# Turning the attention probabilities of the token stage by DMA, as fp16 halves, instead of on TensorE

## What is computed

```python
enc = one_hot(token_ids, 512) + sinusoidal_pe(256, 512)
def layer(enc, ws):
    wq, wk = ws                                   # 512 x 128 each
    q, k = enc @ wq, enc @ wk
    sims = einsum('bqd,bkd->bqk', q, k) / sqrt(128)
    attn = softmax(where(causal_mask, -1e9, sims), axis=-1)
    return einsum('bqk,bkd->bqd', attn, enc), None
enc, _ = lax.scan(layer, enc, (Wq, Wk))           # 4 layers
h = enc
h = h + rwkv_block(layernorm(h))
```

## Time and profile before

| | |
|---|---|
| runs | 2318.48, 2318.91, 2320.64 us |
| profiled execution | 2319.82 us, span 2317.8 us |
| TensorE busy | 2238.2 us, 97% |
| VectorE busy | 1649.5 us, 71% |
| ScalarE busy | 718.5 us, 31% |
| GpSimd busy | 375.0 us, 16% |
| token stage | about 0 to 253 us; RWKV's first matmul at 253.09 |
| TensorE, 150 to 210 us | 47.85 of 60 us busy |
| DMA share, 60 to 150 us | 0.77 |

### The profile page before, as it was taken

How to read it: one execution, slowest core, us unless ns; L and a number is a source line. 1 busy time by engine, 2 the same in 40 slices (tenths; PEclk the granted TensorE clock), 3 DMA queues, 4 the chain that set the end, 5 groups by cost and what they waited for, 6 DMA issues and landing times.

```text
span 2317.8 us, 31891 instructions
## 1 busy us (share of the span) xinstructions
PE 2238.2 (97%) x12058; PEld 1143.5 (49%) x12058; DVE 1649.5 (71%) x3357; ACT 718.5 (31%) x1603; POOL 375.0 (16%) x416
## 2 busy tenths in 40 slices
PE   6777899999999999999999999999999999999999
PEld 4666444444444444444445555554555555444444
DVE  7667799998998886576766666565665667688832
ACT  5676313122122112444333233332333333211111
POOL 3453100000000330541040003100400300400100
PEclk9989999999999999999999999999999999999999
DMA  5866533323332341120131111311311221100001
GB/s 177 257 197 203 212 132 118 125 99 118 132 122 91 142 160 59 44 85 13 50 94 35 35 35 46 89 35 30 95 40 35 66 52 35 59 1 1 1 1 73
DMA packets 171121, 196.60 MB, mean 85 GB/s; under 512 B 124368, under 2 KB 137296, under 8 KB 162000
## 3 DMA queue, kind: packets, MB, share of 16 engines
q1 hardware_dynamic: 170672, 193.41, 27.0%
q10 hardware_dynamic: 288, 1.05, 0.1%
HBM read 137.28 MB, written 27.26 MB: 71 GB/s over the span
## 4 chain that ended last, share of the span: by engine, by line
PE 84%; DVE 6%; issue 3%; ACT 3%; DMA 2%; POOL 2%; SPq 1%; DVEq 0%; ACTq 0%; POOLq 0%
PE ps L749 21%; PE ps L250 14%; PE ps L1370 10%; PE ps L761 7%; PE ps L1173 7%; PE ps L1186 6%; PE ps L642 5%; PE ps L1000 4%; PE ps L1017 3%; PE ps L1211 2%; PE ps L264 2%; PE ps L491 1%; PE ps L607 1%; PE ps L1214 1%; PE ps L262 1%
## 5 line engine op out<-in xcount | busy, mean ns | idle before, releaser
L749 PE MATMUL ps<-planes 128*128 128x512 f16 x1224 | 270.0, 379 | 0.4 <-DVE work L806 0.4
L749 PE MATMUL ps<-planes,wa 128*128 128x512 f16 x1080 | 237.8, 379 | 0.6 <-ACT h L1589 0.6
L250 PE MATMUL ps<-planes,wa 128*128 128x512 f16 x840 | 192.4, 379 | 3.9 <-DVE planes L1727 3.9
L749 PEld LDWEIGHTS ps<-planes 128*128 128x128 f16 x1224 | 119.7, 98 | 142.2 <-DVE work L806 1.2
L250 PE MATMUL ps<-planes 128*128 128x512 f16 x768 | 178.9, 384 | 4.7 <-issue 4.7
L789 ACT ACTIVATE work<-work 128x512 f16<-128x512 f32 x64 | 40.3, 630 | 440.6 <-DVE work L822 440.6
L749 PEld LDWEIGHTS ps<-planes,wa 128*128 128x128 f16 x1080 | 105.6, 98 | 126.1 <-ACT h L1589 1.1
L305 ACT ACTIVATE ps<-ps,nmax 128x128 f32<-128x128 f32 x160 | 54.5, 341 | 307.6 <-DVE nmax L299 307.6
L587 POOL TENSOR_TENSOR rstd<-rstd,half 128x4 f32<-128x4 f32 x16 | 17.5, 1094 | 774.9 <-DVE rstd L582 774.9
L904 DVE COPY_PREDICATED work<-work 128x1024 f32<-128x1024 int16 x144 | 119.6, 831 | 20.9 <-DVE work L904 0.3
L886 DVE TENSOR_SCALAR work<-work,lutx,par 128x256 int32<-128x256 int32 x384 | 128.1, 408 | 0.0
(11 more groups left out here) (195 smaller groups left out, 4247.8 us busy)
## 6 DMA issues: line engine op xcount, KB each, us to landing
planes<-rw SPq DMA_DIRECT2D x17, 2048.0 KB, 8.2
wa<-rw SPq DMA_DIRECT2D x15, 2048.0 KB, 7.5
stg<-in_rw_w SPq DMA_DIRECT2D x32, 512.0 KB, 4.7
stg<-in_ff_w SPq DMA_DIRECT2D x16, 1024.0 KB, 5.1
rw<-wa SPq DMA_DIRECT2D x16, 1024.0 KB, 7.2
stg<-in_mo_w SPq DMA_DIRECT2D x16, 1024.0 KB, 5.5
work<-in_glu_idx SPq DMA_DIRECT2D x48, 128.0 KB, 2.1
glu_dec<-work SPq DMA_DIRECT2D x48, 128.0 KB, 1.7
```

The lines of the kernel that those rows point to most:

```text
L250: mm = te.matmul(ps[:, bank, :], w(i, kt), x(j, kt), start=(kt == 0 and n == 0), stop=(kt == KT - 1 and n == 2))
L749: mm = te.matmul(ps[:, what, :], rw_w(q, what, i, kt, m), mix[what][j][:, kt, at:at + CH], start=(kt == 0 and z == 0), stop=(kt == KT - 1 ...
```

## The change

The probabilities of all units are written by `dve_norm_rows`, so layers 1 to 3 also get a high and a low half, in `prob16`, where the fp32 `prob` was. `sp_prob` turns both with one DMA call of twelve blocks into `pT`, and `tok_pt` waits for it (`pTt_in`). The six transposes, `act_pT` and `dve_pT` are gone. R's rows and columns now lie contiguous, 768 elements of one plane each (`p_turn`), so a turn is two calls of six blocks. In SP's order `sp_prob` of a unit stands at the head of its round, behind the store of the round before, and `sp_pr` follows it. The new layout covers the columns that `load_rw(1)` fills, so this load waits for the last token output and stands behind the last store. In the round of unit (3,1) the first pieces of RWKV's mixing go behind the division of (2,3) and the product of (3,1), on VectorE and ScalarE.

```diff
@@ -120,7 +120,6 @@
 
         qs = [w16(i * 256, CH) for i in range(2)]
         ks = [w16(512 + i * 256, CH) for i in range(2)]
-        prob = w32(1024, 768)
         pT = [w16(1792 + i * 384, 768) for i in range(2)]
         prob16 = [w16(1024 + i * 384, 768) for i in range(2)]
         prob_all = w16(1024, 1536)
...
@@ -264,14 +262,6 @@
                     mm = te.matmul(second, qs[i][:, t0 + P:t0 + S], ks[j][:, t0:t0 + S], start=(n == 0), stop=(n == 2))
             mm.then_inc(scored, 1)
 
-        def pe_transpose_probs(pe, u):
-            pe.wait_ge(probs, u + 1)
-            for b in range(2):
-                for i in range(3):
-                    at = b * 384 + i * P
-                    mm = te.transpose(ps[:, 4 + b, i * P:i * P + P], prob[:, at:at + P], ident[:, :])
-            mm.then_inc(pT_ps, 1)
-
         def act_q(act, u):
             act.wait_ge(q_ps, u + 1)
             se.activation(qs[0], ps[:, 0, :], ACT.Copy, scale=SCALE).then_inc(q_hi, 1)
...
@@ -346,18 +325,7 @@
                 sp.wait_ge(mo_ps, n)
             sp.dma_start_transpose(pT_all, prob_all).then_inc(pT_in, 16)
 
-        pT_view = ps[:, 4:6, 0:384]
-
-        def act_pT(act, u):
-            act.wait_ge(pT_ps, nth(*TOK[u], (1, 2, 3)))
-            se.activation(pT[0].rearrange("p (b k) -> p b k", b=2), pT_view, ACT.Copy).then_inc(pT_hi, 1)
-
-        def dve_pT(dve, u):
-            dve.wait_ge(pT_hi, nth(*TOK[u], (1, 2, 3)))
-            ve.tensor_tensor(pT[1].rearrange("p (b k) -> p b k", b=2), pT_view,
-                             pT[0].rearrange("p (b k) -> p b k", b=2), ALU.subtract).then_inc(pT_split, 1)
-
-
+        pt_view = ps[:, 4:6, 0:384]
 
         TOK = [(0, 0), (0, 1), (1, 0), (0, 2), (1, 1), (2, 0), (0, 3), (1, 2), (3, 0), (2, 1), (1, 3), (2, 2), (3, 1), (2, 3), (3, 2), (3, 3)]
 
...
@@ -375,15 +343,25 @@
 
         TOK_W = wa[:, 8192:16384].rearrange("p (i l q k d) -> p i l q k d", i=2, l=LAYERS, q=2, k=KT)
 
+        def p_turn(half_, c, which):
+
+            at = c * NTOK + CH + which * 768
+            return planes[:, 4 + half_, at:at + 768]
+
         def chunk_rows(half_, c, which):
 
-            return act_T(4 + half_)[:, which:which + 3:2, c * CH:c * CH + 384]
+            return p_turn(half_, c, which).rearrange("p (b k) -> p b k", b=2)
 
         def sp_turn(sp, c, src, done):
             for half_ in range(2):
-                for b in range(2):
-                    dst = act_T(4 + half_)[:, 2 * b + 1 - src, c * CH:c * CH + 384].rearrange("p (n q) -> p n q", n=3)
-                    sp.dma_start_transpose(dst, act_T(4 + half_)[:, 2 * b + src, c * CH:c * CH + 384]).then_inc(done, 16)
+                sp.dma_start_transpose(p_turn(half_, c, 1 - src).rearrange("p (n q) -> p n q", n=6), p_turn(half_, c, src)).then_inc(done, 16)
+
+        def sp_prob(sp, u):
+            n = nth(*TOK[u], (1, 2, 3))
+            sp.wait_ge(probs, u + 1)
+            if n > 1:
+                sp.wait_ge(pt_ps, n - 1)
+            sp.dma_start_transpose(pT_all, prob_all).then_inc(pTt_in, 16)
 
         def sp_p1(sp, u):
             sp.wait_ge(probs, u + 1)
...
@@ -394,18 +372,22 @@
             sp_turn(sp, TOK[u][1], 1, pr_in[TOK[u][1]])
 
         def dve_norm_rows(dve, u):
-            c = TOK[u][1]
+            l, c = TOK[u]
             dve.wait_ge(exps, u + 1)
             ve.reciprocal(rinv[:, :], rsum[:, :]).then_inc(inv_sum, 1)
             dve.wait_ge(inv_sum, u + 1)
-            out = chunk_rows(0, c, 0)
-            low = chunk_rows(1, c, 0)
+            if l == 0:
+                out, low = [chunk_rows(i, c, 0) for i in range(2)]
+            else:
+                out, low = [prob16[i].rearrange("p (b k) -> p b k", b=2) for i in range(2)]
+                if nth(l, c, (1, 2, 3)) > 1:
+                    dve.wait_ge(pTt_in, 16 * nth(l, c, (1, 2, 3)) - 16)
             w = rinv.rearrange("p (i b) -> p i b", i=2)
             ve.tensor_tensor(out[:, :, 0:P], ps[:, 2, 0:S].rearrange("p (b k) -> p b k", b=2),
                              w[:, 0, :].rearrange("p (b k) -> p b k", k=1).to_broadcast([P, 2, P]), ALU.mult)
             ve.tensor_tensor(out[:, :, P:384], ps[:, 3, :].rearrange("p (b k) -> p b k", b=2),
                              w[:, 1, :].rearrange("p (b k) -> p b k", k=1).to_broadcast([P, 2, S]), ALU.mult).then_inc(p1_hi, 1)
-            dve.wait_ge(p1_hi, nth(0, c, (0,)))
+            dve.wait_ge(p1_hi, u + 1)
             for b in range(2):
                 ve.scalar_tensor_tensor(low[:, b, 0:P], ps[:, 2, b * P:b * P + P], rinv[:, b:b + 1],
                                         out[:, b, 0:P], ALU.mult, ALU.subtract)
...
@@ -451,7 +427,7 @@
                 tok_project0(pe, u, c, 1, 1, k_ps)
                 return
             if l == 1:
-                pe.wait_ge(p1T_in[c], 64)
+                pe.wait_ge(p1T_in[c], 32)
             else:
                 pe.wait_ge(pt_lo, nth(l - 1, c, (1, 2, 3)))
             pe.wait_ge(ew_lo, 2 * nth(l - 1, c, (0, 1, 2)))
...
@@ -496,11 +472,13 @@
         def tok_pt(pe, u):
 
             l, c = TOK[u]
-            pe.wait_ge(pT_split, nth(l, c, (1, 2, 3)))
+            pe.wait_ge(pTt_in, 16 * nth(l, c, (1, 2, 3)))
+            if u > 0 and nth(*TOK[u - 1], (1, 2, 3)) > 0:
+                pe.wait_ge(pt_lo, nth(*TOK[u - 1], (1, 2, 3)))
             if l == 1:
                 pe.wait_ge(probs, TOK.index((0, c)) + 1)
             else:
-                pe.wait_ge(pr_in[c], 64 * (l - 1))
+                pe.wait_ge(pr_in[c], 32 * (l - 1))
             for b in range(2):
                 at, t0 = ps[:, 4 + b, :], b * 384
                 for n, (x, y) in enumerate(PASSES):
...
@@ -1552,12 +1530,7 @@
                     tok_out(pe, OUT_AT.index(u))
                 if l < LAYERS - 1:
                     tok_ew(pe, u, 0)
-                if l > 0:
-                    if nth(*TOK[u - 1], (1, 2, 3)) > 0:
-                        pe.wait_ge(pt_lo, nth(*TOK[u - 1], (1, 2, 3)))
-                    pe_transpose_probs(pe, u)
-                else:
-                    pe.wait_ge(probs, u + 1)
+                pe.wait_ge(probs, u + 1)
                 if u in OUT_AT:
                     pe.wait_ge(to_free, outs_before(u + 1))
                 tok_scores(pe, u + 1, 2 * nth(l, c, (0, 1, 2)) - 1 if l < LAYERS - 1 and ew_bank(u, 0) == 2 else 0)
...
@@ -1663,24 +1631,22 @@
                 if l < LAYERS - 1:
                     tok_act_ew(act, u, 0)
                 cols_act(act, COLS_AT.get(u, ()))
-                tok_act_pT(act, u)
                 rw_split_act(act, u)
                 if l < LAYERS - 1:
                     tok_act_ew(act, u, 1)
                 if u == LN_UNIT:
                     ln_chunk(act, mix_act_copy, 0, 0)
                 act_exp(act, u + 1)
-                if u == MU - 4:
-                    mix_hi_act(act, 0)
-                    mix_hi_act(act, 1)
                 if u in ABS_LATE:
                     tok_act_abs(act, ABS_AT.index(u))
                 if l > 0:
                     tok_act_pt(act, u)
+                if u == MU - 4:
+                    mix_hi_act(act, 0)
+                    mix_hi_act(act, 1)
                 if u == MU - 3:
                     mix_hi_act(act, 5)
             u = MU - 2
-            tok_act_pT(act, u)
             mix_hi_act(act, 6)
             act_q(act, u + 1)
             act_k(act, u + 1)
...
@@ -1772,17 +1732,12 @@
                 cols_dve(dve, COLS_AT.get(u, ()))
                 if l < LAYERS - 1:
                     tok_dve_ew(dve, u, 0)
-                tok_dve_pT(dve, u)
                 dve_max(dve, u + 1)
                 if u == 1:
                     cols_lo(dve, COLS_AT[1])
                 if l < LAYERS - 1:
                     tok_dve_ew(dve, u, 1)
-                if u == MU - 4:
-                    mix_diff(dve, 0, 0)
-                    mix_y_dve(dve, 0)
-                    mix_y_dve(dve, 1)
-                tok_dve_norm(dve, u + 1)
+                dve_norm_rows(dve, u + 1)
                 if l > 0:
                     tok_dve_pt(dve, u)
                 if u > 1:
...
@@ -1797,6 +1752,9 @@
                     ve.memset(x_buf(0)[:, :, :, 0:1], 0.0).then_inc(setup_done, 1)
                     ln_chunk(dve, ln_dve_x, 0, 0)
                 if u == MU - 4:
+                    mix_diff(dve, 0, 0)
+                    mix_y_dve(dve, 0)
+                    mix_y_dve(dve, 1)
                     mix_lo_dve(dve, 0)
                     mix_y_dve(dve, 2)
                     mix_lo_dve(dve, 1)
...
@@ -1903,7 +1859,7 @@
                     if q == 0:
                         sp.wait_ge(ew_ps, 2 * (MU - NC))
                     else:
-                        sp.wait_ge(to_ps, 3 * TPC)
+                        sp.wait_ge(to_ps, NT)
                     sp.wait_ge(rw_stored[0], 16 + 16 * (q + 1))
                     sp.wait_ge(rw_stored[1], 16 + 16 * (q + 1))
                 elif q == 2:
...
@@ -1926,6 +1882,10 @@
```

(24 more changed lines are left out.)

30 lines of the change are left out of this document (7 added, 23 removed).

## The result

| | before | after | ratio, 95% interval |
|---|---|---|---|
| first comparison, medians | 2319.41 us | 2340.55 us | 1.0091 [1.0079, 1.0104] |
| second comparison (`after_again`) | 2318.23 us | 2336.78 us | 1.0078 [1.0064, 1.0092] |
| profiled execution (span) | 2319.82 us (2317.8) | 2336.92 us (2334.9) | +17.1 us |

The change makes the kernel 0.8 to 0.9% slower: 18.5 to 21.1 us by the medians, 17.1 by the profiled execution. I had forecast +11.5 (2330, range 2315 to 2342). Direction and place were right, the size was too small. The four executions of the first comparison spread over 6.3 us, so I go by +18.5 and, inside the traces, by +17.1.

A forecast was written before the change was run, and what follows sets the result against it. TensorE's matmuls bound everything from 275 us, so the token stage's delay reaches the end: last unit +8.5 (containing the ring's +4.9), earlier units' landings 0, late weights +3, sum +11.5 us. Forecast 2330 us, range 2315 to 2342.

The forecast's parts named there:

- Removed transposes: Units of layers 1 to 3: dropping six TensorE transposes gains 0 where a VectorE wait follows, 1.0 us at (3,2).
- 1.4 us a low half: VectorE's divisions in layers 1 to 3: each 1.4 us longer, hidden at (1,0), (1,2), (2,0), showing at nine units.
- the ring: Each token unit's loop: scores, mask and maximum (VectorE), exponentials (ScalarE), division (VectorE), `probs`, next scores; lateness was summed along it.
- Relief of SP: SP's queue near 71 us: fewer turn calls issue a load some 7 us earlier, ending ScalarE's 3.18 us wait, -3.2.
- Ledger at the last `probs`: Lateness summed unit by unit through the token stage, reaching +4.9 us at the `probs` of (3,3).
- Last unit: Unit (3,3): `tok_pt` waits for a transpose call issued near 245.1, landing 5.5 us later; +8.5 us, including the earlier +4.9.
- my ends of 3.6 and 9.1: Bounds on the landing time of unit (3,3)'s transpose call, in us, giving +6.6 and +12.1.
- Late load: End of token stage: the 2 MB `load_rw(1)`, held back, delays the index load; +3 us, between 0 and 4.8.
- One sign that I had set for being wrong: Any unit's TensorE waiting over 5 us for `pTt_in` would show the prediction wrong.
- the full queue: Rival: calls of (3,0), (3,1), (3,2) land 6.7 to 9 us after issue; +12 more, 2342 us; chance 12%.
- Relief wins: Rival: all 6.4 us of L357 waits go, low half shows at only two units; -5, 2314 us; chance 13%.
- The estimate of 15.7 us for twelve blocks: Twelve DMA transpose blocks one after another, from the skill's 1309 ns each; it entered only the price-per-block rival, 2410 us, 1%.

The follow-up runs named there:

- after_again: The changed kernel unchanged, timed and profiled a second time beside the kernel before: 2336.78 us, +18.5.
- low_only: Kernel before plus only the low half in the divisions of layers 1 to 3, written to spare memory nobody reads; transposes stay on TensorE: 2333.73 us, +15.6.
- rows_only: Kernel before plus contiguous rows, two transpose calls a turn, and the first 2 MB RWKV weight load behind the last store; probabilities through TensorE: 2321.90 us, +3.8.
- mix_only: Kernel before with only the first mixing work moved behind the division of unit (2,3): 2317.16 us, -1.0.
- rows_mix_idx: Kernel before plus contiguous rows, two-call turns, moved mixing work and index load first; probabilities still by TensorE, no low half: 2314.73 us, -3.5.
- quiet_last_call: Changed kernel with the index load first and unit (3,3)'s transpose call ahead of the last raw load and store: 2328.52 us, +10.3 against before.
- last_call_first: Changed kernel with the store of unit (3,2)'s split weights moved behind the transpose call of unit (3,3): 2334.51 us, ratio 1.0074 against before.

## Why the prediction was right in direction and short in size

- *Removed transposes, about 0.* Right: `probs` and what follows depend on VectorE, and the waits for L357 gave way to others.
- *1.4 us a low half, at nine of twelve units.* The price was right to the tenth. Which units show it was partly wrong: in `low_only` VectorE begins the mask behind (1,0), (1,1) and (2,0) within 0.6 us of before, so (1,1) hides it; so does (3,0), with 0.2 us from its mask to that of (2,1); and at (1,2), which I took as hidden behind ScalarE's transfer, the ring loses 2.4 us there (14.27 from the mask of (1,2) to that of (3,0), before 11.86) and 2.7 in both traces of the changed kernel.
- *Relief of SP, -3.2.* This step failed. The block of calls shrank by 5.2 us, but its worth cannot be seen: `rows_only` and `mix_only` are equally early. I had read a ScalarE wait as a price of the ring without asking whether the ring goes through it. The second trace of the changed kernel has no early lead at (1,2) at all, and a ScalarE wait of 3.6. New calls also took back what was given: `sp_prob` of (1,0) alone holds SP 6.73 us.
- *Ledger at the last `probs`, +4.9.* Measured +11.0 (249.04 against 238.06), 6 short. Of these, 1.0 is the early lead (-1.9 at the mask of (1,2), where I had -2.9), 2.7 is unit (1,2), and some 2.5 came between the mask of (3,0) (+0.8) and the last `probs`: 10.2 where I had 7.7, because the moved mixing gives half of its gain back and unit (2,2) lost 2.9 instead of 1.4, with an enc·W product that took 4.45 us where most take 2.78: the granted clock was 0.62 from 179 to 182 us. In `after_again` that product took 2.78, the unit lost 1.3, and the stretch took 9.5. This item is in part the accident of one execution.
- *Last unit, 5.5 us of landing, +8.5.* The call went out at 250.65 and its product followed 7.4 later, inside my ends of 3.6 and 9.1 but above the value. I took 1.43 us of SP's time; it was 4.08. The +3.6 that the unit adds to the ledger became +4.9.
- *Late load, +3.* The size of the wait was right: it is 3.2 longer. The last store, which `load_rw(2)` and behind it the index load await, landed in 5.35 instead of 3.87, and the index load in 10.43 instead of 8.69. But the clock adds 1.7: the twelve matmuls behind the pause took 4.45 us, not 2.76. `rows_only` shows the same 4.45 behind a wait of 4.21, and +3.8 in total. I had no term for the clock at all.
- The sum by the profiles: 15.9 + 4.9 = 20.8 at the start of L739 (L761 before), of which 17.1 are left at the end. One pause of 2.0 us that the execution before had in a later projection was absent; the other 1.7 I can't place.

One sign that I had set for being wrong was met: a unit, (3,3), waits over 5 us for `pTt_in` (5.95, and (1,0) 5.85 in `after_again`). The product came at 258, not near 251, and the first big matmul at 269, not near 262.

Of the rivals the full queue came nearest in size, but not in place: (3,0), (3,1) and (3,2) waited for nothing, while (1,0), (1,2) and (3,3) waited 2.8, 2.0 and 5.95. "Relief wins" is out: its best form, without the low half and the DMA transposes, is `rows_mix_idx` at -3.5. The rule of the Trainium skill (VectorE: DVE Perf Modes, "Rules for kernel authors"), TensorE for a 128x128 transpose where PSUM will do, chose rightly here. The estimate of 15.7 us for twelve blocks, which I had worked out from its price of one block by DMA ("The three transpose paths"), did not hold: in `quiet_last_call` twelve blocks were used 3.7 us after issue. What decided was VectorE's low half, the queue, and that TensorE had idle time to give away.

## What to carry to other kernels

Work moved off an engine that idles gains nothing; ask first which engine closes the ring, and price what the new path adds there (here 1.4 us of VectorE a unit for an engine that was waiting anyway). Price a DMA by what stands ahead of it in its queue at the moment of issue, not by its median elsewhere, and put small loads on which somebody waits ahead of large ones that are early. Costs that overlap must be taken out together before one is called cheap, and a variant must be timed beside the changed kernel itself.

## What was not expected of the hardware

- Issuing one transpose call of twelve blocks held SP for 1.28 us with a quiet queue (`quiet_last_call`), 1.98 behind a 0.5 MB load alone (`last_call_first`), 4.08 behind a 0.5 MB load and a 1 MB store issued in the microsecond before, and up to 7.20 in unit (1,2). The issue itself stalls, and with it everything behind it on SP.
- A pause of TensorE can cost more than its length, and need not. Twelve matmuls took 2.76 us at the granted clock of 1.00 (2.4 GHz) and 4.45 behind a wait of 3.55, with a clock of 0.63 from 293.4 to 298 us, part of it at the lower level (1.2 GHz). The same twelve took 4.45 behind a wait of 2.73 in `after_again` and 2.76 behind one of 2.79 in `last_call_first`. The last product ran at the lower level in both kernels: its first three matmuls took 0.82 us after and before, and the clock was 0.50 from 250 to 260 us after, from 240 to 250 before.
- Two executions of the same kernel can stand 1 to 3 us apart in the ring for 100 us and more (`after` and `after_again`: +1.9 and +4.8 at (1,3)). One trace does not settle a microsecond there.
